# A scan step's two states added by GpSimd before TensorE sums them

## The reference, cut to what matters

```python
xdbl = jnp.einsum('bld,kd->blk', z, W_xproj)
dt_in, Bm, Cm = jnp.split(xdbl, [DT_RANK, DT_RANK + D_STATE], axis=-1)
dt = jax.nn.softplus(jnp.einsum('blr,dr->bld', dt_in, W_dt) + b_dt)
A_bar = jnp.exp(dt[..., None] * A)
Bx = (dt * z)[..., None] * Bm[:, :, None, :]
# h[l] = A_bar[l] * h[l-1] + Bx[l], along the 36 tokens of an image
y = jnp.einsum('blds,bls->bld', h, Cm) + D_skip * z
```

## Time and profile before

| | us |
|---|---|
| median of 3 runs | 626.87 (625.98 to 630.05) |
| profiled execution | 627.44 |
| its span, first to last instruction | 625.6 |

### The profile page before, as it was taken

The page is one execution under the profiler, slowest core; times in us unless marked ns, Lnnn a source line. Parts: engine busy times, 40 slices in busy tenths (PEclk is TensorE's granted clock), DMA queues, the critical chain, the costliest instruction groups (busy, mean ns, idle before and its releaser), DMA issues.

```text
span 625.6 us, 10398 instructions
## 1 busy us (share of the span) xinstructions
PE 557.0 (89%) x3361; PEld 479.1 (77%) x3361; DVE 475.5 (76%) x897; ACT 295.2 (47%) x699; POOL 388.3 (62%) x447
## 2 busy tenths in 40 slices
PE   3959589977899999989999997999998889978896
PEld 3748478866698988879887885988886768857785
DVE  1166868889789789979879996999989556565664
ACT  1167846483544475544446474445442324323442
POOL 3257777767456458857555984767677355564674
PEclk9779959989899999999999997999999889997999
DMA  9993533432053343413343341554342266553781
GB/s 238 308 299 97 164 119 90 189 135 92 1 155 100 106 155 95 162 33 112 111 171 112 105 141 46 135 157 143 121 177 88 50 207 213 178 174 104 238 274 52
DMA packets 41827, 88.34 MB, mean 141 GB/s; under 512 B 9581, under 2 KB 34477, under 8 KB 35501
## 3 DMA queue, kind: packets, MB, share of 16 engines
q1 hardware_dynamic: 41772, 87.68, 43.4%
HBM read 77.24 MB, written 10.40 MB: 140 GB/s over the span
## 4 chain that ended last, share of the span: by engine, by line
PE 61%; DVE 15%; issue 6%; DMA 6%; ACT 5%; POOL 4%; SPq 2%; POOLq 0%; DVEq 0%; ACTq 0%
PE post L770 12%; PE y_sum L770 10%; PE sums L770 10%; PE gate_up L770 10%; PE pre L770 8%; PE linear_up L770 8%; DVE state L1255 4%; DMA w<-w_store 3%; PE fills L770 3%; DVE fills L1246 2%; DVE dts L1222 2%; SPq L709 1%; POOL read L1456 1%; DMA hid<-patches 1%; DVE scratch L1354 1%
## 5 line engine op out<-in xcount | busy, mean ns | idle before, releaser
L1456 POOL TENSOR_TENSOR read<-state,c_all 128x504 f32<-128x504 f32 (+1 forms) x120 | 147.0, 1228 | 83.2 <-DVE state L1255 54.8
L1255 DVE TENSOR_TENSOR_SCAN state<-a_bar,fills 128x504 f32<-128x504 f32 (+1 forms) x120 | 133.0, 1109 | 12.1 <-ACT a_bar L1035 4.1
L1485 POOL TENSOR_TENSOR scratch<-scratch 128x252 f32<-128x252 f32 (+1 forms) x120 | 81.6, 680 | 87.4 <-DVE scratch L1369 82.4
L770 PE MATMUL y_sum<-read,ident 128*128 128x252 f32 (+1 forms) x480 | 122.5, 382 | 4.1 <-POOL read L1456 3.7
L1035 ACT ACTIVATE scratch<-scratch 128x252 f32<-128x252 f32 (+1 forms) x120 | 47.3, 394 | 147.0 <-DVE scratch L1354 146.8
L770 PE MATMUL sums<-hid,w 128*128 128x252 f32 (+1 forms) x480 | 103.8, 377 | 4.8 <-POOL hid L1494 4.8
L770 PE MATMUL gate_up<-t_high,w 128*128 128x252 f32 (+1 forms) x360 | 89.3, 318 | 14.5 <-DVE route L1332 7.2
L770 PEld LDWEIGHTS y_sum<-read,ident 128*128 128x128 f32 x480 | 86.3, 201 | 19.8 <-issue 7.1
L1035 ACT ACTIVATE a_bar<-dts,decay 128x245 f32<-128x245 f32 (+1 forms) x240 | 100.2, 470 | 2.2 <-DVE dts L1230 2.2
L1494 POOL TENSOR_TENSOR hid<-scratch,route_rows 128x252 f32<-128x252 f32 (+1 forms) x120 | 84.9, 708 | 14.4 <-DMA route_rows<-mix_rows 7.6
L770 PE MATMUL linear_up<-t_high,w 128*128 128x252 f32 (+1 forms) x360 | 85.8, 308 | 2.3 <-ACT mix_w L1035 1.7
(11 more groups left out here) (166 smaller groups left out, 851.9 us busy)
## 6 DMA issues: line engine op xcount, KB each, us to landing
w<-w_store SPq DMA_DIRECT2D x40, 1152.0 KB, 5.7
route_rows<-mix_rows SPq DMA_DIRECT2D x192, 63.0 KB, 3.0
w_store<-w SPq DMA_DIRECT2D x8, 1152.0 KB, 5.0
scratch<-expert_w SPq DMA_DIRECT2D x16, 384.0 KB, 5.6
w<-expert_w SPq DMA_DIRECT2D x1, 2304.0 KB
route_rows<-mix_rows SPq DMA_DIRECT2D x48, 36.0 KB, 2.8
w_embed<-embed_w SPq DMA_DIRECT2D x3, 256.0 KB, 3.9
x_patch<-patches SPq DMA_DIRECT2D x1, 756.0 KB, 5.0
```

The costliest lines, as they stand in the source:

```text
L770: return nc.tensor.matmul(out, lhsT, rhs, start=start, stop=stop, skip_group_check=shared, is_transpose=turned)
L1255: dve.tensor_tensor_scan(pair(state, i, c), pair(a_bar, i, c), pair(fills, i, c), 0.0, ALU.mult, ALU.add).then_inc(scanned.sem, 1)
L1456: pool.tensor_tensor(by_state(pair(read, i, c)), by_state(pair(state, i, c)), c_all[:, n:n + 2, 0:tok(c)], ALU.mult).then_inc(read_out.sem, 1)
L1485: pool.tensor_tensor(glu[:, 0:tok(c)], product[un % 2][:, 0:tok(c)], g_one[un % 2][:, 0:tok(c)], ALU.mult)\
```

## The change

GpSimd gets a new step `fold` per scan step: it adds the second half of a `read` slot onto the first, in place. `collect` is then one matmul over that half instead of two. `collect` waits for `fold`, and `fold` for the `read` of the same step. In the order, `fold` of step i-1 stands in the turn of `advance` i, ahead of `read` i. The last `fold` of a cut stands behind the first two turns of the next cut's scan; the collects of steps 22 and 23 and the last `y` stay where they were. The model gets a price for `fold` and half the price for `collect`, and six constants of the order have new values. Nothing else changes.

```diff
-        turns += [ahead + [("drive_b", i)], [("advance", i), ("read", i)]]
+        turns += [ahead + [("drive_b", i)], [("advance", i)] + ([("fold", i - 1)] if i else []) + [("read", i)]]
...
-    return [[("collect", SCAN_STEPS - 2)], [("collect", SCAN_STEPS - 1)], [("y", NJ - 1)]]
+    return [[("fold", SCAN_STEPS - 1)], [("collect", SCAN_STEPS - 2)], [("collect", SCAN_STEPS - 1)], [("y", NJ - 1)]]
...
-                "read": [("advance", i), ("collect", i - READ_SLOTS)], "collect": [("read", i)]}[step]
+                "read": [("advance", i), ("collect", i - READ_SLOTS)], "fold": [("read", i)], "collect": [("fold", i)]}[step]
...
-            turns = turns[:first - 2] + ends + turns[first - 2:]
+            turns = turns[:2] + ends[:1] + turns[2:first - 2] + ends[1:] + turns[first - 2:]
...
-    "advance": (("V", 1.13),), "read": (("G", 1.2),), "collect": (("P", .85),), "y": (("V", .43),),
+    "advance": (("V", 1.13),), "read": (("G", 1.2),), "fold": (("G", .68),), "collect": (("P", .43),), "y": (("V", .43),),
...
-WAIT_WEIGHT = 0.5
-BEFORE_SPAN = 15.5
-AFTER_SPAN, LAST_AFTER_SPAN = 20.9, 22.0
-EXPERT_SPAN, LAST_EXPERT_SPAN = 25.1, 21.7
+WAIT_WEIGHT = 1.44
+BEFORE_SPAN = 16.07
+AFTER_SPAN, LAST_AFTER_SPAN = 18.93, 17.82
+EXPERT_SPAN, LAST_EXPERT_SPAN = 22.86, 22.8
...
-                pe.wait_ge(read_out.sem, read_out.at(c, i + 1))
-                for k in range(2):
-                    last = mm(half(y_sum, c, 0), ident[:, :], half(read[:, i % READ_SLOTS, :], c, k),
-                              r == 0 and k == 0, r == STEPS_PER_BLOCK - 1 and k == 1)
-                last.then_inc(pe_y.sem, 1)
+                pe.wait_ge(folded.sem, folded.at(c, i + 1))
+                mm(half(y_sum, c, 0), ident[:, :], half(read[:, i % READ_SLOTS, :], c, 0),
+                   r == 0, r == STEPS_PER_BLOCK - 1).then_inc(pe_y.sem, 1)
...
+            def fold(c, i):
+                pool.wait_ge(read_out.sem, read_out.at(c, i + 1))
+                one, two = (half(read[:, i % READ_SLOTS, :], c, k) for k in range(2))
+                pool.tensor_tensor(one, one, two, ALU.add).then_inc(folded.sem, 1)
```

More of the change, by code:

```diff
@@ L226, in rests_on @@
                 "x_scale": [("x_glu", i)], "x_down": [("x_scale", 2 * (i // 3) + 1)]}[step]
-    if step in ("decay", "fill", "drive_b", "advance", "read", "collect"):
+    if step in ("decay", "fill", "drive_b", "advance", "read", "fold", "collect"):
         return {"decay": [("advance", i - A_SLOTS)], "fill": [("advance", i - FILL_SLOTS)], "drive_b": [("fill", i)],
                 "advance": [("drive_b", i), ("decay", i), ("read", i - STATE_SLOTS)],
-                "read": [("advance", i), ("collect", i - READ_SLOTS)], "collect": [("read", i)]}[step]
+                "read": [("advance", i), ("collect", i - READ_SLOTS)], "fold": [("read", i)], "collect": [("fold", i)]}[step]
     return None
@@ L557, in vit_tower @@
         read_out = signal("read_out", SCAN_STEPS)
+        folded = signal("folded", SCAN_STEPS)
         pe_y = signal("pe_y", SCAN_STEPS)
@@ L1512, in _ @@
             run({"scale": scale, "power": power, "power2": power2, "power3": power3, "split_w1": split_w1,
-                 "drive": drive, "read": read_states, "outproj": outproj, "scale3": scale3, "h1": h1, "t_low": t_low_rest, "x_glu": x_glu,
+                 "drive": drive, "read": read_states, "fold": fold, "outproj": outproj, "scale3": scale3, "h1": h1, "t_low": t_low_rest, "x_glu": x_glu,
                  "x_scale": x_scale})
```

## The result

The changed kernel takes 639.3 us (637.8 to 640.5) beside 626.6 for the kernel before on the same chip: a ratio of 1.019, 95% interval 1.015 to 1.023. It is slower; 607 was forecast, in a range that ended at 628.

The account below looks back on a forecast made before the run. PE was taken to bound the three full scans, DVE close behind. Terms -15 (full scans), -2.5 and +2 (before them), -5 (moved places), +0.5 (end) gave -20 us: 607 us, range 586 to 628.

Parts of the forecast that it names:

- The moved places: Routing of cut 3 about four scan steps earlier, taking about four units out of the tail: -5 us, ends -10 and 0.
- the full scans: Stretches of cuts 2, 3 and 4: DVE becomes fullest, at 95.5%, so 310 us become 295: -15 us.
- three signs of being wrong: Scans not shortening while PE shows idle time; `x_gated` past 1.1 us; clock falling in the full stretches.
- x_gated: DVE operation delayed by folds on POOL: mean 783 ns to near 0.87 us, 2 us a full stretch, ends 0 and 3.7.
- the rival in which all 34 us of PE arrive: Whole kernel: PE stays the bound, saving 30.6 us in the full stretches and 3.4 before: 591 us, chance 0.12.
- The second rival: DVE bounds at once, PE's saving becomes idle PE, full stretches give nothing: 625 us, chance 0.20.
- put the clock at 0: Full stretches: PE, at about 92% after the change, keeps its upper clock level; cost 0.
- Cover: POOL's 83.2 us idle right before `read` is there to take 81.7 us of folds.
- The sum by stretch: POOL's busy time with folds in the three full stretches: 80.7, 89.6 and 88.0 us, below DVE.
- The wait: `collect` waits for `fold`, there a turn early: cost 0, up to 8.6 us; at the very end +0.5.
- Before the full stretches: From 62 to 101 us folds fill POOL to 37.5 of 39 us: +2, ends 0 and +5; 101 to 132: -2.5.
- The slower rival: Three full stretches: folds hold `x_gated` on DVE; at 1.35 us each +15 us, 637 in all, chance 0.13.

Follow-up runs that it names:

- e5: Changed kernel's instruction order with the work of the kernel before (no fold, two matmuls a step that wait for `read`): 647.7 us, ratio 1.035.
- e15: Kernel before with the new `WAIT_WEIGHT` (1.44) and nothing else: 643.9 us, ratio 1.026.
- e3: Changed kernel's order, no fold, one matmul a step that waits for `read`, second state left out of the sum: 636.6 us, ratio 1.017.
- e7: Order of the kernel before, no fold, one matmul a step that waits for `read`, second state left out of the sum: 616.0 us, ratio 0.984.
- e6: Order of the kernel before with each fold put ahead of the next `read` and one matmul a step that waits for the fold: 639.5 us, ratio 1.019.
- e11: Order of the kernel before with folds and one matmul in cuts 2 to 4 alone, two matmuls in cuts 0 and 1: 627.9 us, ratio 1.001.

## Why the prediction was wrong

Two steps failed. The moved places were put at -5 us and the new `WAIT_WEIGHT` at nothing, without a word; with the old work the new order costs 21 us (e5), and the weight alone 16 (e15). And DVE was to fill the full scans to 95.5% once PE was relieved; it stays at 89%, and the relief is worth 10 to 11 us where 17.5 were forecast. In the prediction's own stretches, us of one profiled execution each, up to 4 off its median (the forecast with the moved units' work counted into the scans):

| | to the last `y` of cut 1 | three full scans | behind them | sum |
|---|---|---|---|---|
| forecast | -0.5 | -9 | -10.3 | -20 |
| measured | +18.4 | +6.8 | -12.0 | +13.1 |
| new order with the old work (before to e5) | +14.9 | +20.4 | -13.9 | +21.5 |
| one matmul less in it (e5 to e3) | +0.9 | -13.7 | +1.7 | -11.1 |
| folds in it (e3 to after) | +2.6 | 0.0 | +0.1 | +2.7 |
| one matmul less, old order (before to e7) | -1.6 | -6.1 | -2.8 | -10.4 |
| folds, old order (e7 to e6) | +16.8 | +8.2 | +1.8 | +26.8 |

Two of the prediction's three signs of being wrong came: the scans don't shorten while PE shows idle time, and the clock in the three stretches shown above falls to 0.89, 0.97 and 0.93 (1.00, 1.00 and 0.97 before). The third, `x_gated` past 1.1 us, didn't.

*Which engine bounds, and what PE's relief is worth.* The three full scans were said to give 15 us and the stretch before them 2.5. The relief alone, without folds, is worth 10.3 in the old order and 11.1 in the new; nothing of it in the head (161.4 to 160.7). So the rival in which all 34 us of PE arrive is refuted, and the forecast's own 17.5 was too much even with POOL's part left out. "DVE's waits were mostly on the engine that is relieved" was the reason for 95.5%; but its waits for `gate_up` and `linear_up`, 58.2 us before, are still 48.7 in e7 and 51.9 after. The second rival, a saving that turns into idle PE, came nearest in mechanism, but DVE isn't full either, and its 625 has no price for the order. What is new with less work on PE is a lower granted clock: 0.89 to 0.79 from 43 to 165 us (before and e7 above), 0.945 to 0.913 over the span. I had put the clock at 0. How much of the missing relief is the clock's, no run separates.

*Cover.* "POOL stands idle for 83.2 us right before `read`" was read as room for 81.7 us of folds. That idle time is 47.8 us less after the change. The sum by stretch ("80.7, 89.6 and 88.0 us: below DVE") was nearly right (78.9, 93.1 and 89.7) and what follows from it depends on the order. In the new order, laid out with the fold in its model, the cover held: folds and their wait cost 2.7 us, nothing of it in the full scans. POOL is over 7.4 us busy there in 10 of the 27 slices of 8 us from 264 to 480 (the kernel before: 2), but DVE is over 7.7 in each of these ten. In the old order, from which the 83.2 us were read, it failed: the folds take back more than PE's relief gives.

*The wait.* "There a turn early: cost 0, up to 8.6" failed in the scans of cuts 0 and 1 and held in the full ones. Two waits of the changed kernel, and one of DVE:

```profile
PEld y_sum L771 <- POOL read L1461: 15.4, 12, 4.6
PE y_sum L771 <- POOL read L1461: 13.8, 11, 4.4
DVE fills L1245 <- PE fills L771: 13.4, 11, 3.7
```

Of PE's 13.8 us all but 0.5 lie before 155 us. A turn early in the order is no time when the queue in between is full. What stood behind the waiting instruction, `fills`, I hadn't named; but DVE waited 7.6 us for `fills` before the change too, and its longest wait after it (3.69 us, up to 107.28) has no stand for a fold just ahead of it. Together the folds' time and this wait cost the changed kernel 2.7 us (e3 to after), inside what was forecast for them; in the old order the wait takes up to 11 of the 23.5 us that the folds cost.

*Before the full stretches.* POOL was forecast at 37.5 of 39 us from 62 to 101, "too full for a queue in order", and priced at +2, at most +5. For the old order the place was right and the size wrong: it loses 15.6 us in the head (e6). In the changed kernel the stretch to the last `y` of cut 1 loses 18.4, but 14.9 of it is the new order's (e5) and 2.6 the folds'.

*The moved places.* The step of -5 (0 to -10) is the worst: +21. Its tail is right: four units at 2.7 us, 10.8, measured 12.0. What the same work costs among the scans was priced by DVE's time alone, 4 x 1.6 us; with the old work the scans grow by 28.8 (e5). And it looked only at the units of cut 3 and gave `WAIT_WEIGHT` no price, while the weight moved steps in all cuts (e15: +8.1 in the head, +7.7 in the scans, the tail the same). Which moved steps hold up which, beyond that, I haven't found.

*`x_gated`.* It was to go from 783 to about 870 ns in the last scan. After, by shape, from 394 to 494 us, against the earlier trace rows:

```profile
L1368 DVE SCALAR_TENSOR_TENSOR scratch<-scratch 128x252 f32<-128x252 f32 x24 | 19.1, 797 | 0.8
```

So +14 ns, and over the span 634 to 629. The slower rival (held at 1.35 us, 637) named a time near the measured one by a mechanism that isn't there.

*How the pieces add.* They don't: the order alone costs 21 us, the folds with their wait 23.5 (e7 to e6), and both together with PE's relief 12.7 net. With folds in, either order ends at 639 (e6, after). Two ways of telling the loss are thus both true: the folds cost more than the relief in the old order, and the new order, in which they cost 2.7, costs about as much by itself. No single step of the change is "the" cause; that the relief is only 10 to 11 us, less than the folds cost in the one order and less than the other order costs, holds in both.

## What to carry to other kernels

A queue's idle time before one instruction, summed over a kernel, is not by itself room for new work: read the queue in slices about two steps long, and ask in each what else stands in it. Before an addition moves from a full engine to a slack one, measure the relief alone (leave the work out) and the load alone (do it for nobody): two runs would have told here that 10 us are to be had and at least 12 to be paid. And where a program orders the work, a changed weight is a change of its own, to be timed with the old work.

## What was not expected of the hardware

Taking matmuls away lowered the granted clock where the other engines' busy time in that stretch stayed as it was (0.89 to 0.79, e7), and PE's busy time fell by only 5.8 us in 122 with 91 records fewer. The new order shows the same: 0.923 to 0.871 over the span from e5 to e3. In the changed kernel from 65 to 88 us, where the kernel before has 0.74 in the same window:

```profile
65.00:88.00 23.00, 11.57 (x39) 9.71 (x38) 16.57 (x26) 16.22 (x40) 20.11 (x26) 0.54 0.40 135
```

There POOL is busy for 20.11 of 23 us and PE for half, at 0.54; the matmuls left cost more each (`y_sum` 382 to 430 ns over the span).

The lock of VectorE's and GpSimd's ports that the Trainium skill, "SBUF — State Buffer", section "SBUF: two separate sides", describes would let 85 us of further two-input additions on POOL lengthen `x_gated`. No run here shows that: 783 and 797 ns in the last scan, and 741 and 718 ns from 268 to 490 us in e7 and e11, without and with folds. Single long instances remain, but folds did not add to them by any sum that counts. Folds are lengthened themselves, in single cases: three of the 24 small ones of the changed kernel take 1.07 to 1.26 us (78.92, 80.87 and 85.58), each beside an operation of DVE on `dts`.
